# A two-layer graph attention kernel: the row of r made in every partition from raw e1, and the maxima of e2 carried by the same transfer

## The reference, cut to what matters

```
h   = relu(layernorm(x))
Wh  = h @ W                          # 1024 x 128
e1, e2 = Wh @ a1, Wh @ a2            # one number of each for every node
e   = leaky(e1[i] + e2[j])           # slope 0.2, 1024 x 1024
att = softmax(where(adj, e, -big), over j)
x   = x + elu(att @ Wh)              # layer 0
x   = x + att @ Wh                   # layer 1
```

## Time and profile before

| what | value |
|---|---|
| median of three runs | 290.95 us (290.85 to 292.67) |
| the profiled execution, its own time | 291.18 us |
| its span, first to last instruction | 289.4 us |
| TensorE busy | 285.1 us, 99% |
| VectorE busy | 254.4 us, 88% |
| ScalarE busy | 195.1 us, 67% |
| GpSimd busy | 79.7 us, 28% |
| DMA, mean busy share | 77% of 16 engines, 292 GB/s |
| granted TensorE clock | 1.0 of full in every slice |

### The profile page before, as it was taken

One profiled execution on the slowest core, in us unless ns is written; L12 is line 12 of the kernel. 1 busy time (PEld: TensorE's weight loads), 2 busy tenths in 40 slices (PEclk: granted clock), 3 DMA queues, 4 the chain that ended last, 5 costly groups with the idle time before them and its releaser, 6 DMA issues.

```text
span 289.4 us, 6600 instructions
## 1 busy us (share of the span) xinstructions
PE 285.1 (99%) x2523; PEld 284.2 (98%) x2523; DVE 254.4 (88%) x493; ACT 195.1 (67%) x534; POOL 79.7 (28%) x143
## 2 busy tenths in 40 slices
PE   7999999999999999999999999999999999999996
PEld 7999999999999999999999999999999999999995
DVE  3898899898989989898998979979797997779986
ACT  4686795995959679495886929569292865916400
POOL 2412705315071420706035070512407042000000
PEclk9999999999999999999999999999999999999999
DMA  7999659597795949679287896959769596896922
GB/s 235 418 407 407 243 183 408 216 371 298 260 413 163 415 170 359 278 245 412 76 315 286 291 378 204 404 186 389 294 243 410 166 409 250 313 406 205 374 104 75
DMA packets 25387, 84.52 MB, mean 292 GB/s; under 512 B 3966, under 2 KB 5132, under 8 KB 25356
## 3 DMA queue, kind: packets, MB, share of 16 engines
q1 hardware_dynamic: 24780, 83.70, 76.8%
q10 hardware_dynamic: 576, 0.39, 0.4%
HBM read 79.83 MB, written 4.26 MB: 291 GB/s over the span
## 4 chain that ended last, share of the span: by engine, by line
PE 99%; POOL 0%; DVE 0%; issue 0%; POOLq 0%
PE acc L1041 76%; PE prj L957 9%; PE tp L887 5%; PE acc L1056 2%; PE acc L876 2%; PE acc L937 1%; PE tp L976 1%; PE prj L1056 1%; PE prj L927 1%; PE prj L1041 1%; PE tp L970 1%; PE tp L896 0%; PE tp L993 0%; PE tp L985 0%; PE acc L896 0%
## 5 line engine op out<-in xcount | busy, mean ns | idle before, releaser
L1041 PE MATMUL acc<-wh,pbuf 128*128 128x129 f32 x1968 | 227.6, 275 | 0.0
L1041 PEld LDWEIGHTS acc<-wh,pbuf 128*128 128x128 f32 x1968 | 224.0, 192 | 0.1
L734 DVE SCALAR_TENSOR_TENSOR pbuf<-row_r,sqr,adj_sb 128x1024 f32<-128x1024 f32 x125 | 154.8, 1277 | 2.9 <-ACT row_r L483 2.9
L498 ACT ACTIVATE accs<-accs,rec 128x128 f32<-128x128 f32 x120 | 36.6, 388 | 26.7 <-DVE rec L770 26.7
L320 POOL TENSOR_TENSOR mean<-stats 128x8 f32<-128x8 f32 x14 | 11.7, 836 | 142.9 <-DVE stats L632 139.5
L433 ACT ACTIVATE xn<-x_sb,shift,rstd 128x128 f32<-128x128 f32 x120 | 47.7, 479 | 0.0
L466 ACT ACTIVATE wh<-prj,wh 128x128 f32<-128x128 f32 x120 | 32.8, 363 | 0.0
L483 ACT ACTIVATE row_r<-in_row 128x1024 f32<-128x1024 f32 x14 | 29.4, 2098 | 2.4 <-DMA in_row<-row_mem 2.4
L957 PE MATMUL prj<-w_ext,hT 128*128 128x130 f32 x240 | 29.3, 275 | 0.0
L957 PEld LDWEIGHTS prj<-w_ext,hT 128*128 128x128 f32 x240 | 28.0, 191 | 0.0
L347 POOL TENSOR_TENSOR rstd<-vareps,neg_half 128x8 f32<-128x8 f32 x15 | 26.0, 1731 | 6.9 <-DVE vareps L651 5.8
(11 more groups left out here) (114 smaller groups left out, 181.1 us busy)
## 6 DMA issues: line engine op xcount, KB each, us to landing
adj_sb<-in_adj SPq DMA_DIRECT2D x64, 1024.0 KB, 10.7
in_row<-row_mem SPq DMA_DIRECT2D x7, 641.0 KB, 4.3
x_sb<-in_x SPq DMA_DIRECT2D x7, 512.0 KB, 11.5
in_row<-row_mem SPq DMA_DIRECT2D x7, 512.0 KB, 4.3
out_x<-x_sb SPq DMA_DIRECT2D x7, 512.0 KB, 12.9
x_sb<-in_x ACTq DMA_DIRECT2D x1, 256.0 KB, 3.6
x_sb<-in_x SPq DMA_DIRECT2D x1, 256.0 KB, 3.5
row_mem<-sqr SPq DMA_DIRECT2D x14, 4.0 KB
```

Of the source, the lines that this page charges most:

```text
L498: op = nc.scalar.activation(hp[:, t, :], hp[:, t, :], ACT.Copy, scale=rec[:, t:t + 1])
L734: nc.vector.scalar_tensor_tensor(pbuf[:, t, :], row_r[:, n % 2, :], sqr[:, n % 2, 0, t:t + 1], adj_at(n, t), ALU.max, ALU.min).then_inc(p_ ...
L1041: mm = nc.tensor.matmul(sum_at(k, s), pbuf[:, t, i * P:(i + 1) * P], wh[:, n % 2, t, :], start=(t == 0 and s == 0 and k < NB), stop=(t == ...
```

## The change

For the stages from 2 on, e1 and e2 are copied out of prj into e_pair, e1 in row 0 with the partition's maximum of e2 as a ninth number beside its eight. These nine numbers of each partition go to memory as soon as they are there, and one transfer brings all 1152 into every partition. VectorE finds M from the 128 maxima in the loaded row (exp_args_later), at a new place in its order: before mask 7. ScalarE makes s and q (exps_later), then r for all nodes with two instructions over 1024 numbers (make_row: Relu with M as the bias, which also sorts, and Exp in place), and only then scales Wh. The last column of Wh moves to GpSimd (last_column), the copy of u from ScalarE to VectorE, and spread_emax, zrow, the small exp for r, sort_row and mask_unsorted are gone for these stages. make_row reads in_row with a step of 9 numbers (36 bytes).

```diff
+        e_pair = sb("e_pair", [P, 2, T + 1])
+        e_row = e_pair[:, 0, :]
+        e2 = e_pair[:, 1, 0:T]
...
-        in_row = sb("in_row", [P, N + 2 * C])
-        row_by_node = in_row[:, 0:N]
-        u_rows = in_row[:, N:N + 2 * C].rearrange("p (s c) -> p s c", s=2)
...
+        ROW = N + P
+        in_row = sb("in_row", [P, ROW + 2 * C])
+        row_parts = in_row[:, 0:ROW].rearrange("q (p t) -> q t p", t=T + 1)
+        u_rows = in_row[:, ROW:ROW + 2 * C].rearrange("p (s c) -> p s c", s=2)
...
             def load_row(m):
                 k = loaded_rows(m)
-                if m % 2 == 1:
-                    sp.wait_ge(u_copied, m // 2)
-                    sp.wait_ge(row_in, 16 * (k - 1))
-                    sp.dma_start(row_mem[N:N + 2 * C].rearrange("(s c) -> s c", s=2),
-                                 u_sums[:, :]).then_inc(r_written, 16)
-                sp.wait_ge(r_known, m + 1)
+                sp.wait_ge(emax_ready, m + 1)
                 if k > 1:
                     sp.wait_ge(row_in, 16 * (k - 1))
-                sp.dma_start(row_mem[0:N].rearrange("(p t) -> p t", t=T),
-                             sqr[:, m % 2, 2, :]).then_inc(r_written, 16)
+                sp.dma_start(row_mem[0:ROW].rearrange("(p t) -> p t", t=T + 1),
+                             e_row).then_inc(r_written, 16)
+                if m % 2 == 1:
+                    sp.wait_ge(u_copied, m // 2)
+                    sp.dma_start(row_mem[ROW:ROW + 2 * C].rearrange("(s c) -> s c", s=2),
+                                 u_sums[:, :]).then_inc(r_written, 16)
                 sp.wait_ge(r_written, 16 * written(m))
                 if k > 1:
                     sp.wait_ge(row_sorted, k - 1)
                 sp.wait_ge(acc_copied, NB * (m - 1))
                 if m % 2 == 0:
-                    sp.dma_start(row_by_node, row_mem[0:N].partition_broadcast(P)
+                    sp.dma_start(in_row[:, 0:ROW], row_mem[0:ROW].partition_broadcast(P)
                                  ).then_inc(row_in, 16)
                 else:
                     sp.dma_start(in_row[:, :], row_mem.partition_broadcast(P)).then_inc(row_in, 16)
...
+            def last_column(m):
+                pool.wait_ge(q_known, m + 1)
+                nc.gpsimd.tensor_scalar(wh[:, m % 2, :, D], sqr[:, m % 2, 1, :], Q_SCALE, None,
+                                        ALU.mult).then_inc(q_ready, 1)
...
                 normaliser(m)
+                if m > 2:
+                    last_column(m - 1)
+            last_column(LAST)
...
+            def exps_later(m):
+                act.wait_ge(args_ready, m + 1)
+                nc.scalar.activation(sqr[:, m % 2, 1, :], from_max[:, :], ACT.Exp,
+                                     scale=SLOPE).then_inc(q_known, 1)
+                nc.scalar.activation(sqr[:, m % 2, 0, :], from_max[:, :], ACT.Exp,
+                                     scale=1.0 - SLOPE).then_inc(sqr_ready, 1)
...
-            def sort_row(m):
+            def make_row(m):
                 k = loaded_rows(m)
                 act.wait_ge(row_in, 16 * k)
+                act.wait_ge(cmax_ready, m + 1)
                 act.wait_ge(p_ready, T * (m - 1))
                 nc.scalar.activation(row_r[:, m % 2, :].rearrange("q (t p) -> q t p", t=T),
-                                     row_by_node[:, :].rearrange("q (p t) -> q t p", t=T),
-                                     ACT.Copy).then_inc(row_sorted, 1)
-            def copy_u(n):
-                k = n // 2
-                act.wait_ge(upair_done, k)
-                if k > 1:
-                    act.wait_ge(r_written, 16 * written(n - 1))
-                nc.scalar.activation(u_sums[:, 0:D], UPAIR, ACT.Copy,
-                                     scale=EMPTY).then_inc(u_copied, 1)
+                                     row_parts[:, 0:T, :], ACT.Relu,
+                                     bias=cmax[:, 0:1]).then_inc(row_added, 1)
+                act.wait_ge(row_added, k)
+                nc.scalar.activation(row_r[:, m % 2, :], row_r[:, m % 2, :], ACT.Exp,
+                                     scale=SLOPE - 1.0).then_inc(row_sorted, 1)
...
@@ -554,26 +575,15 @@
                 elu = stages[n - 1][0] == 0
                 if n == LAST:
                     seed_last()
-                if n < LAST and not elu:
-                    if n % 2 == 0:
-                        copy_u(n)
-                    exps(n + 1)
                 scale_accs(n - 1)
                 if n < LAST:
                     if elu:
-                        if n % 2 == 0:
-                            copy_u(n)
-                        exps(n + 1)
                         elu_exp(n - 1)
                     if n + 2 <= LAST:
                         normalise(n + 2)
-                    early = T // 2 if elu else T
-                    scale_wh(n + 1, range(early))
-                    sort_row(n + 1)
-                    if early < T:
-                        scale_wh(n + 1, range(early, T))
+                    exps_later(n + 1)
+                    make_row(n + 1)
+                    scale_wh(n + 1)
                 if n + 2 <= LAST:
                     copy_hT(n + 2)
...
-                if m == 1:
-                    nc.vector.tensor_scalar(uniform[:, m % 2, 0:D], USUM, EMPTY, None,
-                                            ALU.mult).then_inc(e_copied, 1)
+                nc.vector.tensor_scalar(uniform[:, m, 0:D], USUM, EMPTY, None,
+                                        ALU.mult).then_inc(e_copied, 1)
                 dve.wait_ge(e_copied, e_copies(m))
                 nc.vector.tensor_reduce(emax[:, :], ecol[:, :, 1], AX_X, ALU.max).then_inc(emax_ready, 1)
+            def copy_e_later(m):
+                dve.wait_ge(prj_done, m + 1)
+                full = prj[:, 0:2, 0:NB * E].rearrange("p b (s e) -> p b s e", e=E)[:, :, :, D:E]
+                nc.vector.tensor_copy(e_pair[:, :, 0:2 * NB].rearrange("p e (b s) -> p b s e", b=2),
+                                      full).then_inc(e_copied, 1)
+                part = prj[:, 2, 0:tiles_in[2] * E].rearrange("p (s e) -> p s e", e=E)[:, :, D:E]
+                nc.vector.tensor_copy(e_pair[:, :, 2 * NB:T].rearrange("p e t -> p t e"),
+                                      part).then_inc(e_copied, 1)
+                dve.wait_ge(e_copied, e_copies(m))
+                nc.vector.tensor_reduce(e_row[:, T:T + 1], e2, AX_X,
+                                        ALU.max).then_inc(emax_ready, 1)
+            def copy_u(n):
+                k = n // 2
+                dve.wait_ge(upair_done, k)
+                if k > 1:
+                    dve.wait_ge(r_written, 16 * written(n - 1))
+                nc.vector.tensor_scalar(u_sums[:, 0:D], UPAIR, EMPTY, None,
+                                        ALU.mult).then_inc(u_copied, 1)
...
+            def exp_args_later(m):
+                dve.wait_ge(row_in, 16 * loaded_rows(m))
+                nc.vector.tensor_reduce(cmax[:, :], row_parts[:, T, :], AX_X,
+                                        ALU.max).then_inc(cmax_ready, 1)
+                dve.wait_ge(cmax_ready, m + 1)
+                nc.vector.tensor_scalar(from_max[:, :], e2, cmax[:, 0:1], None,
                                         ALU.subtract).then_inc(args_ready, 1)
...
-            def mask_unsorted(n):
-                dve.wait_ge(adj_in[n % ADJ_SLOTS][0], 16 * (n // ADJ_SLOTS + 1))
-                dve.wait_ge(p_used, n)
-                dve.wait_ge(row_in, 16 * loaded_rows(n))
-                nc.vector.scalar_tensor_tensor(
-                    pbuf[:, 0, :].rearrange("q (t p) -> q t p", t=T),
-                    row_by_node[:, :].rearrange("q (p t) -> q t p", t=T),
-                    sqr[:, n % 2, 0, 0:1],
-                    adj_at(n, 0).rearrange("q (t p) -> q t p", t=T),
-                    ALU.max, ALU.min).then_inc(p_ready, 1)
-                dve.wait_ge(row_sorted, loaded_rows(n))
...
@@ -842,27 +867,24 @@
                 l, b = stages[n - 1]
                 masks(n, range(DRAIN))
                 take_acc(n - 1)
-                copy_e(n + 1)
-                if l == 0:
-                    masks(n, (DRAIN,))
-                    exp_args(n + 1)
-                else:
-                    exp_args(n + 1)
-                    masks(n, (DRAIN,))
-                masks(n, range(DRAIN + 1, 6))
+                copy_e_later(n + 1)
+                if n % 2 == 0:
+                    copy_u(n)
+                masks(n, range(DRAIN, 6))
                 if l == 0:
                     add_elu(b)
                     masks(n, (6,))
                     add_x(b)
+                    exp_args_later(n + 1)
                     masks(n, (7,))
                 else:
                     add_hp(b)
-                    masks(n, (6, 7))
+                    masks(n, (6,))
+                    exp_args_later(n + 1)
+                    masks(n, (7,))
                 if n + 3 <= LAST:
                     statistics(n + 3)
```

(12 more changed lines are left out.)

8 lines of the change are left out of this document (5 added, 3 removed).

## The result

The changed kernel is slower: a ratio of 1.0349 with an interval of 1.0305 to 1.0392 against 291.07 us, which is 301.2 us. Of its six executions (median 301.7) three took 300.6 to 300.8 us, two 302.6 and 302.9, and one 1043.71, which the ratio leaves out. The prediction was 297.6 with a range of 292.5 to 301.5; the narrower range of the forecast's own mechanism was 295.8 to 300. The profiled execution took 300.61 us with a span of 298.8, and the kernel before 291.18 with 289.4: +9.4 us, where the working had +6.6.

The account below looks back on a forecast made before the run. TensorE, busy 99%, was taken as the bound. Removing spread_emax saves 1.5 us, waits add 7.2 in layer 0, 0.4 in layer 1, 0.5 at the end: +6.6, 297.6 us in medians; range 292.5 to 301.5.

Parts of the forecast that it names:

- the forecast's own mechanism: TensorE waits nearly a microsecond for hT in each of eight stages of layer 0; 297.6 us, chance 0.63.
- second rival: The row through memory comes last in layer 1: five stages lose 0.7 us, the last a little more; 301, chance 0.12.
- Steps 1 to 4: Layer 0 stage: copies, masks, loaded row hidden, arguments at S + 8.61 (even 8.8), Relu 0.85 us after they start.
- Step 5: make_row's Relu over 1024 numbers with a step of 36 bytes: bounds 1.06 and 2.10 us, 2.10 taken.
- first rival: The Relu isn't slowed by its step (1.06 us), layer 0 doesn't wait, only the 1.5 us saving stays: 289.5, chance 0.13.
- Steps 6 and 7: ScalarE's Exp 0.97 us, GpSimd's last column hidden, scale_wh 2.00, copy_hT 1.16; project waits 0.92 or 0.89 us, 7.2 over eight stages.
- Layer 1: Stages n = 9 to 13: hT 0.2 us early, but the row can be late; 0.4 us in all, bounds 0 and 3.5.
- The last stage: Stage 15's first mask needs the sorted row, so stage 14's first bank comes late for TensorE: 0.4 to 0.5 us.
- third rival: ScalarE's tail is some tenths shorter or VectorE reaches the arguments earlier, 0.4 us less per layer 0 stage: 294.5, chance 0.12.

Follow-up runs that it names:

- a2: The changed kernel with make_row's Relu reading its first 1024 numbers in a line, without the sorting; ratio 1.0386 to the kernel before, 302.5 us.
- a3: The changed kernel with the stores of the seven graphs issued behind the loop; ratio 1.0248 to the kernel before, span 296.6 us.
- two of the first experiments: On the changed kernel: the exps' arguments moved before mask 6 and add_x behind layer 0 (297.6 us), and a2 (302.5 us).

## Why the prediction was right, and where it was off

The sign, the mechanism and the place of the largest term held; the sizes were too small. Layer 0 waits for hT behind a chain of exactly the steps that were listed, +7.23 us net where the working gave 7.2 less 0.9 for the saved transposes; TensorE's saving is real (stages 9 and 10 are 0.11 shorter each) and lost wherever it waits. Against the working's +6.6 us of span the +9.4 is 0.9 more in layer 0, 1.4 more in layer 1, 0.8 more at the end, and 0.2 less before stage 1. 301.2 lies above the forecast's own range (to 300) and inside the wide one (to 301.5) by 0.3 us, because the wide one took in the second rival; with an interval that reaches 302.5, that is partly luck. By steps:

- **Steps 1 to 4** (the way to the arguments): right within 0.05 us, copy_u's 0.2 among them, and only the maximum over strided numbers (0.37 for 0.28) was taken too short. In layer 0 the row was there in time.
- **Step 5**, the Relu at sort_row's price: 2.16 us for 2.10, right. The first rival is out: a2 shows 1.14 without the step, so the row with 32 bytes was the right one to read. The Trainium skill ("SBUF — State Buffer", section "Specifications (TRN2)": cachelines of 16 bytes, two hits in a line for full bandwidth, a penalty for each new line) told the same, and both measurements agree with it.
- **Steps 6 and 7**: right within 0.03. The chain as a whole was 0.11 longer, 0.9 us over eight stages. The Exp, the last column on GpSimd (0.96, hidden) and the order behind them were as drawn.
- **Layer 1**: the term that was mis-sized. "I count 0.4 us for all five stages" came from the latencies of the kernel before, with 3.26 us as the longest write. In the changed kernel the writes took 3.0 to 3.74 in stages 11 to 14, and stages 11 to 13 grew by 1.47 us, TensorE's saving of 0.3 already taken off. This is the second rival's mechanism: the write stands closer to the transfers of the stage before, and a3, which takes the stores away, removed all of it. "All transfers of a stage move ahead together" was the wrong argument against it: in stage 11 the write was issued 1.36 us earlier and the load, with all that stands behind it in the queue, 0.30. A likely reading, from the stage lengths alone and not tried apart: stages 9 and 10 are a us shorter than those before, so the row of stage 11 catches up with transfers that were started at the pace of longer stages.
- **The last stage**: 1.16 us where 0.4 net was forecast. The row was later (maximum at S + 8.25, not 7.9), and the two masks ended at S + 15.0, not 14.4. With the stores out of the way (a3) 0.6 is left of the 1.16. TensorE stood 1.14 us for the first bank of stage 14; in the timeline after, the masks, the banks and TensorE's wait (its idle time is in the waits above):

```profile
278.39 2.48 DVE L772 SCALAR_TENSOR_TENSOR pbuf<-row_r,sqr,adj_sb 128x1024 f32<-128x1024 f32 x2 [2.43 <-ACT row_r L513]
...
280.79 1.35 DVE L785 TENSOR_TENSOR accs<-acc,in_row 128x387 f32<-128x387 f32 x3
...
281.49 1.58 PE L1058 MATMUL acc<-wh,pbuf 128*128 128x129 f32 x12 [1.14 <-DVE accs L785]
```

- **The third rival** is out: nothing of ScalarE's tail was shorter than the rows had it, and VectorE reached the arguments at S + 8.60 for the 8.61 forecast.
- **What wasn't seen**: GpSimd. The prediction used it only for the last column. Its shift had ended 0.6 us before mask 2 in the changed kernel (69.91 + 0.20 against 70.70, stage 3 above), so the forecast wasn't hurt; but an engine that isn't on the path made two of the first experiments come out otherwise than the theory said. In the kernel before shift met mask 2 in the even stages too and was out at its end. There exp_args follows that mask, here in stage 4:

```profile
86.23 1.27 DVE L734 SCALAR_TENSOR_TENSOR pbuf<-row_r,sqr,adj_sb 128x1024 f32<-128x1024 f32 x1
87.43 0.28 DVE L697 TENSOR_REDUCE cmax<-tp 128x1 f32<-128x128 f32 x1
```

VectorE doesn't pause where mask 2 ends (87.50); the maximum out of PSUM is running when shift ends at 87.57. And copy_u is on ScalarE in that kernel. Both differences came with the change, and either can be why shift was never held longer there.

## What to carry to other kernels

Before moving a value behind a transfer, count the whole serial tail that then stands between the transfer's first reader and the next input of the bound engine, here 7.3 us from the maximum to project, and compare it with the room that the consumer has; a tenth of a us saved on the bound engine isn't worth a tail that is longer than the room. When a change reorders small instructions of VectorE, look at the GpSimd instructions beside them: two small copies with waits between masks 2 and 3, 0.3 us in all, were worth 5 us here (297.6 to 292.6). And a small write that is on the path should not be issued behind transfers that nobody waits for: here stores of half a megabyte each, put behind the loop, gave back 2.2 us of span (a3).
